# First cross attention: scores from rounded halves and remainders in fp32r instead of plain fp32

## The reference

```python
rq = (iQ @ Wq.T).reshape(b, q, H, ADIM)
kv = (iK @ Wkv.T).reshape(b, s, 2, H, ADIM)
rk, rv = (kv[:, :, 0], kv[:, :, 1])
scores = jnp.einsum('bqhd,bshd->bhqs', rq, rk) / sqrt(ADIM)
scores = jnp.where(mask[:, None, :, :], jnp.float32(-1e+32), scores)
attn = sparse_norm(scores, nbias)      # t = relu(s + nbias) ** 2, t / (sum t + 1e-32)
o = jnp.einsum('bhqs,bshd->bqhd', attn, rv).reshape(b, q, H * ADIM)
return o @ Wo.T
```

## Time and profile before

| what | value |
|---|---|
| median of 3 runs | 955.69 us (952.36 to 958.51) |
| the profiled execution, its own time | 957.4 us |
| its span, first to last instruction | 955.7 us |
| mean granted TensorE clock | 0.983 of full |
| TensorE matmul busy | 909.0 us, 95% |
| VectorE busy | 630.7 us, 66% |
| ScalarE busy | 500.7 us, 52% |
| score matmuls (L543) | 37.6 us busy, 1024 records |

### The profile page before, as it was taken

How to read it: one execution, slowest core, us unless ns; L and a number is a source line. 1 busy time by engine, 2 the same in 40 slices (tenths; PEclk the granted TensorE clock), 3 DMA queues, 4 the chain that set the end, 5 groups by cost and what they waited for, 6 DMA issues and landing times. The chain is left out here.

```text
span 955.7 us, 20196 instructions
## 1 busy us (share of the span) xinstructions
PE 909.0 (95%) x8260; PEld 745.7 (78%) x8260; DVE 630.7 (66%) x866; ACT 500.7 (52%) x721; POOL 197.2 (21%) x190
## 2 busy tenths in 40 slices
PE   8999999887989998989999999999999999998996
PEld 7888888755669997569898999999988877567554
DVE  5667776668734345599797989798979752376222
ACT  5777777544466663665554565646464541312331
POOL 2000000020214441422221331404050210421101
PEclk9999999899989999999999999999999999997999
DMA  5211110020212321548877888787979780899993
GB/s 162 78 63 50 49 50 5 3 67 0 70 46 80 95 88 58 163 132 229 245 196 235 218 245 222 219 239 223 236 223 255 211 233 4 276 337 260 342 337 115
DMA packets 103848, 151.92 MB, mean 159 GB/s; under 512 B 11009, under 2 KB 84434, under 8 KB 103762
## 3 DMA queue, kind: packets, MB, share of 16 engines
q1 hardware_dynamic: 102930, 148.35, 53.4%
q0 software_dynamic: 832, 2.36, 0.8%
HBM read 114.50 MB, written 36.18 MB: 158 GB/s over the span
## 5 line engine op out<-in xcount | busy, mean ns | idle before, releaser
L189 PE MATMUL ps<-f_pT_hi,f_cN_hi 128*128 128x256 f32 x512 | 146.4, 286 | 5.4 <-DVE f_pT_lo L1898 5.3
L189 PE MATMUL ps<-f_pT_lo,f_cN_hi 128*128 128x256 f32 x512 | 147.7, 288 | 0.0
L189 PE MATMUL ps<-f_pT_hi,f_cN_lo 128*128 128x256 f32 x512 | 146.0, 285 | 0.0
L448 DVE SCALAR_TENSOR_TENSOR a_u<-ps,a_floor,a_cap 128x1024 f32<-128x1024 f32 x64 | 79.2, 1279 | 48.2 <-PE ps L543 47.8
L189 PEld LDWEIGHTS ps<-f_pT_hi,f_cN_hi 128*128 128x128 f32 x512 | 97.1, 190 | 9.7 <-DVE f_pT_lo L1898 7.9
L1749 POOL TENSOR_TENSOR f_cN_lo<-e_raw,f_cN_hi 128x512 fp32r<-128x512 f32 x32 | 49.7, 1578 | 262.0 <-ACT f_cN_hi L1776 262.0
L189 PEld LDWEIGHTS ps<-f_pT_hi,f_cN_lo 128*128 128x128 f32 x512 | 98.8, 193 | 0.0
L189 PEld LDWEIGHTS ps<-f_pT_lo,f_cN_hi 128*128 128x128 f32 x512 | 97.2, 190 | 1.0
L1898 DVE TENSOR_TENSOR f_pT_lo<-f_pT_lo,f_pT_hi 128x1024 fp32r<-128x1024 f32 x64 | 81.4, 1297 | 23.9 <-ACT f_pT_hi L1785 23.9
L359 ACT ACTIVATE a_pr<-a_u,a_nb 128x1024 f32<-128x1024 f32 x64 | 73.8, 1153 | 43.7 <-DVE a_u L448 42.5
L1785 ACT CAST f_pT_hi<-f_pT_lo 128x1024 fp32r<-128x1024 f32 x64 | 66.8, 1049 | 55.0 <-DMA f_pT_lo<-f_turned_rows 54.9
(11 more groups left out here) (414 smaller groups left out, 2180.9 us busy)
## 6 DMA issues: line engine op xcount, KB each, us to landing
f_turned_rows<-f_turned SPq DMA_DIRECT2D x64, 512.0 KB, 4.5
f_pT_lo<-f_turned_rows SPq DMA_DIRECT2D x256, 128.0 KB, 3.3
k_w<-in_L_ffn_W SPq DMA_DIRECT2D x30, 1024.0 KB, 14.8
a_ctxT<-in_ctxT SPq DMA_DIRECT2D x16, 512.0 KB, 4.5
d_w<-in_L_ffn_w SPq DMA_DIRECT2D x32, 256.0 KB, 2.7
e_raw<-in_ctxT SPq DMA_DIRECT2D x8, 1024.0 KB, 8.0
e_raw<-in_ctx SPq DMA_DIRECT2D x32, 256.0 KB, 6.2
k_b<-in_L_ffn_b SPq DMA_DIRECT2D x14, 256.0 KB, 11.2
```

Source lines behind the costliest of these rows:

```text
L189: last = nc.tensor.matmul(out, a[i], b[j], start=start and n == 0, stop=stop and n == 2, skip_group_check=skip)
L448: V.scalar_tensor_tensor(u[:, n % NU, :].rearrange("p (r w) -> p r w", r=RT), core.psum[:, 0:2048].rearrange("p (r w) -> p r w", r=RT)[:, ...
```

## The change

The keys `kT` and the laid-out queries `qd` become pairs of fp32r tiles, the rounded half and the remainder. ScalarE's `evict` and `queries` now write the rounded halves. VectorE gets two new duties: `key_rest(m)` subtracts the rounded keys from the piece that still lies in PSUM, once for each of the four key pieces of a batch, and `query_rest(b)` makes the two remainders of the queries of a batch. `scores` takes three accumulating passes of four row tiles instead of one plain fp32 pass of four. A piece now waits, besides the eviction, for `key_rest` of the piece two before (same bank), and `scores` of a batch's first tile waits for all its remainders.

```diff
-        kT = [sb(f"kT{i}", [P, DC, S]) for i in range(2)]
+        kT = [[sb(f"kT{i}_{n}", [P, DC, S], F32R) for n in ("hi", "lo")] for i in range(2)]
-        qd = [sb(f"qd{i}", [P, DC, HR, T]) for i in range(2)]
+        qd = [[sb(f"qd{i}_{n}", [P, DC, HR, T], F32R) for n in ("hi", "lo")] for i in range(2)]
...
+            def key_rest(m):
+                b, n = m // PIECES, m % PIECES
+                if n >= 4 or b >= B:
+                    return
+                c, cols = n % 2, slice(512 * (n // 2), 512 * (n // 2) + 512)
+                dve.wait_ge(kv_ready, m + 1)
+                V.tensor_tensor(kT[b % 2][1][:, c, cols], core.bank(4 + n % 2), kT[b % 2][0][:, c, cols].bitcast(F32),
+                                ALU.subtract).then_inc(k_lo, 1)
+
+            def query_rest(b):
+                for g in range(HR):
+                    dve.wait_ge(qd_ready, HR * b + g + 1)
+                    V.scalar_tensor_tensor(qd[b % 2][1][:, :, g, :], qT[:, :, b * T:(b + 1) * T], pairmask[:, g:g + 1],
+                                           qd[b % 2][0][:, :, g, :].bitcast(F32), ALU.mult, ALU.subtract
+                                           ).then_inc(qd_lo, 1)
...
             remainder_weights(1)
+            key_rest(0)
+            key_rest(1)
             dve.wait_ge(x_in, 16)
             norm.vector_norm(dve, step, x, core.xn, LN_EPS, norm.xn)
+            key_rest(2)
+            key_rest(3)
             norm.vector_transposed(dve)
...
+            query_rest(0)
             limits(0)
             clamp(0)
+            key_rest(PIECES)
             clamp(1)
+            key_rest(PIECES + 1)
             for b in range(B):
                 for j in range(KT // 2):
                     for i in range(2):
                         n = KT * b + 2 * j + 2 + i
                         if n < LAST:
                             clamp(n)
+                        key_rest(PIECES * (b + 1) + 2 * j + 2 + i)
+                    if j == 2 and b + 1 < B:
+                        query_rest(b + 1)
                     if j < DC and b + 2 < B:
                         remainder(b + 2, j)
...
                 if m >= 2:
                     pe.wait_ge(kv_ready, m - 1)
+                    pe.wait_ge(k_lo, 4 * ((m - 2) // PIECES) + min((m - 2) % PIECES + 1, 4))
...
                 if k == 0:
                     pe.wait_ge(kv_ready, PIECES * b + 4)
-                    pe.wait_ge(qd_ready, DC * (b + 1))
+                    pe.wait_ge(k_lo, 4 * b + 4)
+                    pe.wait_ge(qd_lo, HR * (b + 1))
...
-                    for r in range(RT):
-                        rows = slice(32 * r, 32 * r + 32)
-                        last = t.matmul(core.bank(r)[:, first:first + P],
-                                        kT[b % 2][rows, c, k * P:(k + 1) * P],
-                                        qd[b % 2][rows, c, :, :].rearrange("p h t -> p (h t)"), start=True, stop=True)
+                    for i, h in enumerate(((0, 0), (0, 1), (1, 0))):
+                        for r in range(RT):
+                            rows = slice(32 * r, 32 * r + 32)
+                            last = t.matmul(core.bank(r)[:, first:first + P],
+                                            kT[b % 2][h[0]][rows, c, k * P:(k + 1) * P],
+                                            qd[b % 2][h[1]][rows, c, :, :].rearrange("p h t -> p (h t)"),
+                                            start=i == 0, stop=i == 2)
```

More of the change, by code:

```diff
@@ L247, in xattn0 @@
         v_ones, wo_zero, ident_ready = sem("v_ones"), sem("wo_zero"), sem("ident_ready")
+        k_lo, qd_lo = sem("k_lo"), sem("qd_lo")
         o_ready, y_psum, x_out = sem("o_ready"), sem("y_psum"), sem("x_out")
@@ L329, in queries @@
                 for g in range(HR):
-                    A.activation(qd[b % 2][:, :, g, :], qT[:, :, b * T:(b + 1) * T], ACT.Copy,
+                    A.activation(qd[b % 2][0][:, :, g, :], qT[:, :, b * T:(b + 1) * T], ACT.Copy,
                                  scale=pairmask[:, g:g + 1]).then_inc(qd_ready, 1)
@@ L340, in evict @@
                         act.wait_ge(s_psum, KT * (b - 1))
-                    A.copy(kT[b % 2][:, c, 512 * h:512 * h + 512], bank).then_inc(kv_ready, 1)
+                    A.copy(kT[b % 2][0][:, c, 512 * h:512 * h + 512], bank).then_inc(kv_ready, 1)
                 else:
```

## The result

The changed kernel takes 996.36 us (median of 4, 994.17 to 1002.9), the kernel before 957.1 us (median of 4, 952.36 to 959.4): a ratio of 1.043, 95% interval 1.036 to 1.050. It is slower by some 39 us; 997 was forecast. Slow executions (two of the kernel before, at 4976 us, and one of its variant with the early division, at 964) are left out of all medians and ratios.

What follows compares the result with a forecast made beforehand. TensorE was taken to bound the first block, with VectorE's division ending almost together with its list at j = 3. Terms 11.4 + 15.8 + 4.9 + 8.5 = 40.6 us gave 997 us, own range 985 to 1012.

Steps and rivals of the forecast that it cites:

- 26 pairs: Score pairs on TensorE's list: twelve load slots instead of eight, +0.44 us a pair, 11.4 us in all.
- 5 waits: At j = 3 of batches 1 to 5 the next outputs wait for VectorE's late division: 3.15 us each, 15.8 us.
- the start: Before and just after the first scores: piece 4 waits for a remainder behind the layer norm; 4.9 us together.
- the clock: TensorE's clock falls to half for 3.4 us after five of six waits: 8.5 us.
- the loads bind and the waits don't: Rival: VectorE and ScalarE have more slack at j = 3 than the timeline shows; 972 us, chance 0.08.
- The plain fp32 rate at 128 columns: Rival: in the scores each fp32r pass costs what the one plain pass did, 24 slots a pair; 1031 us, chance 0.07.
- The one that is not slower: Rival: passes decide the scores' time and the remainders find VectorE idle; 951 us, chance 0.08.

Runs made afterwards that it cites:

- its variant with the early division: The kernel before with the division moved from step j = 3 to j = 1 on VectorE; 956.4 us, ratio 0.996.
- halved loads: The changed kernel, but the second and third score pass load only 64 of their 128 key columns as weights; 985.7 us in one execution.
- halved columns: The changed kernel, but the second and third score pass move only 64 of their 128 query columns; 996.6 us in one execution.
- the early division: The changed kernel with the division of the batch before moved from step j = 3 to j = 1 on VectorE; 979.5 us, ratio 1.023.
- without remainders: The changed kernel with three score passes, all rounded half by rounded half, and no remainders made or waited for; 972.9 us, ratio 1.016.
- one pass: The changed kernel with all remainders made and waited for, but only the first of the three score passes; 981.6 us, ratio 1.025.
- Filling the waits: The changed kernel, but TensorE fills its wait before the outputs of batches 2 to 6 with eleven unread matmuls; 989.4 us, ratio 1.033.

## Why the prediction was right

The mechanisms were the forecast ones; the four terms of the sum, each by its trace:

| term | forecast, us | measured, us |
|---|---|---|
| 26 pairs | 11.4 | 10.1 |
| 5 waits | 15.8 | 14.8 |
| the start | 4.9 | 5.1 |
| the clock | 8.5 | 6.3 |
| sum | 40.6 | 36.3 (the block: 36.3) |

- **The price of the scores.** A slot is 0.11 us, twelve a pair, as taken from the L2739 row. What was too high is the rest: the 0.21 us beside the slots were kept, and a pair took 1.49, which is 12 x 0.111 and 0.16. (The prediction puts this rest down to filling and emptying the array; no run takes it apart.) So 26 x 0.39. The halved loads and the halved columns show that the load binds. By the four passes that the Trainium skill gives true fp32 (page "FP8 and Floating Point Precision", section TensorE Precision Notes), taken alone, a pair would have come to 0.88 us; the 1.49 measured speaks against counting passes here, since the load hides what they save.
- **The remainders on VectorE.** Forecast 8.5 us from `outputs` to `outputs`, measured 8.30; the remainder ended at 81.69, 5.57 after the start of the step (5.7), the division at 8.14 (8.35). 5 x (8.30 - 5.35) = 14.8. Both runs of one part alone confirm it: without remainders no wait, with remainders and one pass the same 8.4. The rival by which the loads bind and the waits don't is refuted by the five waits of 2.7 us in the trace, and by the early division, which ended them by nothing but another order.
- **The start.** Piece 4 at 17.90 (forecast 17.85), the first scores 4.56 us late (4.35), the third piece behind them by 0.49 (0.6). From the norm on the path is the forecast one, but agreement this close is luck: the first remainders began late because the context came late, and the second did not wait for its eviction as forecast. In the other traces with the same start piece 4 starts between 17.27 and 18.35 us, and the first scores between 29.8 and 32.1.
- **The clock.** Four falls behind five waits and none at the start, in place of five of six. From the pair of scores ahead of a wait to the one behind it are 10.32 us with a fall (80.13 to 90.45) and 8.75 without (third wait, 133.97 to 142.72), so a fall costs 1.57 and four 6.3. Filling the waits agrees (6.6 in all). It was the least founded term, a count of cases, and that it came out within some 2 us is partly luck: in the run with one pass all five waits and the start had falls, and in the run with halved columns, whose waits are as long as these, the clock was low in the block for twice the time.
- **The other rivals.** The plain fp32 rate at 128 columns didn't show: one record a matmul, 0.11 us a slot, and 0.06 behind a halved load. The one that is not slower would have needed the division at 4.9 us in the step; it ended at 8.14.
- **The end point.** The medians differ by 39.3 us, the two profiled executions by 37.1, the forecast was 40.6. Within the spread of the executions of one kernel (7 to 9 us) these agree. That 997 and 996.36 lie within 1 us is luck: the sum was 4.3 us above what the block shows, and the medians differ by 3 us more than the block.

Why the change lost: it saves passes, and loads set the pace. How long a plain fp32 pass is shows in the kernel before where 256 columns move (TensorE, timeline of the last batch, two short windows):

```profile
186.23 0.59 PE L578 MATMUL ps<-a_wo,a_oT 128*128 128x256 f32 x2
186.44 0.59 PE L578 MATMUL ps<-a_wo,a_oT 128*128 128x256 f32 x2
```

One record follows the other after 0.21 us, so one of 128 columns takes an estimated 0.11, as long as its load of 0.111. Two such records became three shorter passes, but each pass still brings its own load, so two loads became three. To get the remainders that the passes need, it put work on an engine with 6 idle us a batch, but in front of the one instruction for which TensorE already waited.

## What to carry to other kernels

Where the pass of a matmul is shorter than its load, count loads, not passes. Here a load of 128 weight columns takes 0.111 us and a pass of 256 fp32r columns 0.12, so by estimate this holds up to some 240 moved columns. Splitting an fp32 product into three passes should pay only where each load serves more columns than that; no run here tries it. Before giving work to an engine with idle time, write out its list for the step and ask what stands behind the new instruction and for what it must wait; here half of the loss, and the clock with it, came back by moving one division two steps earlier. Here a wait that starved TensorE for 2.7 us cost 1.6 us more than its length wherever the clock fell behind it.

## What was not expected

- Five idle stretches of TensorE of the same 2.71 to 2.72 us were followed by a clock at 0.50 four times and by a full clock once (135.5 to 138.2 us); in the run with one pass, with waits of 3.7 us, it fell five times in five. The length of the wait alone does not decide it: in the run with halved columns, with waits of 2.74 us, it also fell five times in five, and in the run with halved loads, with waits of 3.1 us, three times in five.
- With loads of 64 columns beside loads of 128 in one stream, a group starts 0.06 or 0.11 us after the one before, by the size of the load before; a pair takes 0.1 to 0.2 us more than its slots.
- The kernel before itself lost some 3 to 4 us (ratio 0.996, 0.993 to 0.999) to the place of one division.
